# Fewer sweeps and a double-buffered activation tile in a three-stage transformer block on eight cores

## What is computed

```python
x = x + 0.5 * ffn(layernorm(x))
x = x + attn(layernorm(x))[0]      # attn returns x' + cfc_out @ out_w.T + out_b
x = x + 0.5 * ffn(layernorm(x))

def ffn(x):                        # both matrices ternary, activations 8 bit
    h = bit_linear(x, w1)                          # 1024 -> 4096
    h = silu(depthwise_conv1d(h, conv_w, conv_b))  # 3 taps along the sequence
    return bit_linear(h, w2)                       # 4096 -> 1024
def bit_linear(x, w):              # act_quant divides by the row's scale again
    return einsum('bsd,hd->bsh', act_quant(x), weight_quant(w))

def attn(x):                       # layernorm, a state space scan, then per step:
    def step(h, xt):
        cat = concatenate([xt, h], -1)
        ff1 = tanh(cat @ ff1_w.T + ff1_b); ff2 = tanh(cat @ ff2_w.T + ff2_b)
        t = sigmoid((cat @ ta_w.T + ta_b) * 0.1 + (cat @ tb_w.T + tb_b))
        return ff1 * (1 - t) + t * ff2             # h_new
```

## Time and profile before

| | us |
|---|---|
| median of 3 runs (lowest, highest) | 8986.92 (8979.69, 8989.06) |
| the profiled execution | 8987.16 |
| its span, slowest core (core 6) | 8985.6 |
| spans of the 8 cores | 8943.4 to 8985.6 |
| mean granted TensorE clock of the cores | 0.687 to 0.690 |

### The profile page before, as it was taken

The page is one execution under the profiler, slowest core; times in us unless marked ns, Lnnn a source line. Parts: engine busy times, 40 slices in busy tenths (PEclk is TensorE's granted clock), DMA queues, the critical chain, the costliest instruction groups (busy, mean ns, idle before and its releaser), DMA issues. The chain is left out here.

```text
span 8985.6 us, 55001 instructions; the slowest of 8 cores (8943.4 to 8985.6 us)
## 1 busy us (share of the span) xinstructions
PE 3672.7 (41%) x17501; PEld 1967.2 (22%) x17682; DVE 3800.5 (42%) x7133; ACT 2088.6 (23%) x3546; POOL 64.3 (1%) x119
## 2 busy tenths in 40 slices
PE   0223323332333210666322178888832332333257
PEld 0122212221222110323100033333410221222123
DVE  2445454554455441000465444444434545454400
ACT  2222222222222213000000015555510222222200
POOL 0000000000000000000000000000000000000000
PEclk9756655665666555878655589999965665566578
DMA  7000000000000024232111100000033000000132
GB/s 205 31 28 14 14 16 27 14 14 19 24 14 14 24 70 154 82 105 95 56 52 51 64 19 1 1 1 1 1 137 115 14 15 14 28 14 14 33 126 84
DMA packets 310172, 406.89 MB, mean 45 GB/s; under 512 B 20482, under 2 KB 224514, under 8 KB 304130
## 3 DMA queue, kind: packets, MB, share of 16 engines
q1 hardware_dynamic: 296546, 341.50, 12.1%
q0 software_dynamic: 13344, 61.87, 2.2%
HBM read 271.23 MB, written 135.26 MB: 45 GB/s over the span
## 5 line engine op out<-in xcount | busy, mean ns | idle before, releaser
L467 PE MATMUL pb<-xq,wq 128*128 128x258 bf16 x3584 | 660.2, 370 | 1041.7 <-DVE tg L494 659.2
L467 PE MATMUL pb<-xqb,wq 128*128 128x258 bf16 x3072 | 568.2, 371 | 972.2 <-DVE tg L494 596.5
L566 PE MATMUL pb<-yqb,wq 128*128 128x512 bf16 x3511 | 801.8, 389 | 374.7 <-DMA yqb<-yqbuf 249.2
L467 PEld LDWEIGHTS pb<-xq,wq 128*128 128x128 bf16 x3584 | 465.6, 132 | 1241.1 <-issue 1075.0
L486 DVE SCALAR_TENSOR_TENSOR tg<-pb,convws,tg 128x256 f32<-128x256 f32 x832 | 345.1, 478 | 901.3 <-ACT tg L478 887.2
L851 PE MATMUL pb<-cfc,WhS 128*128 128x512 bf16 (+1 forms) x2880 | 677.1, 364 | 87.5 <-DVE cfc L882 47.8
L467 PEld LDWEIGHTS pb<-xqb,wq 128*128 128x128 bf16 x3072 | 400.2, 133 | 1144.7 <-issue 1001.2
L478 ACT ACTIVATE tg<-pb,convbs,convws 128x256 f32<-128x256 f32 x832 | 401.3, 562 | 748.0 <-PE pb L467 546.9
L572 DVE SCALAR_TENSOR_TENSOR yy<-pb,rw2h,xt 128x512 f32<-128x512 f32 x112 | 84.1, 751 | 1091.8 <-PE pb L566 1091.8
L566 PEld LDWEIGHTS pb<-yqb,wq 128*128 128x128 bf16 x3584 | 356.8, 100 | 816.4 <-issue 414.5
L532 DVE TENSOR_TENSOR yqa<-y,pbc 128x256 bf16<-128x256 f32 x832 | 280.3, 414 | 548.1 <-ACT y L527 548.1
(11 more groups left out here) (176 smaller groups left out, 4523.1 us busy)
## 6 DMA issues: line engine op xcount, KB each, us to landing
yqb<-yqbuf SPq DMA_DIRECT2D x9, 4096.0 KB
yqbuf<-yqa SPq DMA_DIRECT2D x34, 1024.0 KB
yqb<-yq2buf SPq DMA_DIRECT2D x5, 4096.0 KB
xt<-xT SPq DMA_DIRECT2D x9, 2048.0 KB
x1buf<-yy SPq DMA_DIRECT2D x9, 2048.0 KB
yq2buf<-yqa SPq DMA_DIRECT2D x18, 1024.0 KB
xta<-xT SPq DMA_DIRECT2D x17, 1032.0 KB
y<-w1T SPq DMA_DIRECT2D x8, 2048.0 KB
```

Of the source, the lines that this page charges most:

```text
L467: mm = T.matmul(pb[j][:, 0:tw], wq[:, kd * HD + mh * P:kd * HD + (mh + 1) * P], xq_t[:, kd * tw:(kd + 1) * tw], start=(kd == 0), stop=(kd ...
L566: mm = T.matmul(bank[:, 0:tw], wq[:, kh * D + md * P:kh * D + (md + 1) * P], yqb[:, kh * tw:(kh + 1) * tw], start=(kh == 0), stop=(kh == H ...
```

## The change

Four things are edited.

1. `NSWEEP` goes from 18 to 15. Since 15 is odd, the states of the last sweep go to the second half of `cfc`, and the output projection reads those of the 14th sweep.
2. Stage A no longer copies the scales into `a2col`.
3. Stage B no longer spreads them: the `tensor_scalar` instructions that fill `repb`, the four transposes and the copy into `a1s` of each tile are gone.
4. Stage B gets two buffers for `yqb`. The load of a tile moves from the SP queue to the GpSimd queue (`G.dma_start`), and that of tile i+1 is issued at the start of tile i, once VectorE and TensorE have finished tile i-1. TensorE waits for `yqb` alone. SP still waits for the last eviction and for the store of `yy`, and then issues `xt`; VectorE waits for it. `xt` and `yy` stay single.

```diff
-NSWEEP = 18
+NSWEEP = 15
...
-                quant_cols(y2, HC, TOA, None, 2,
-                           acol_dst=a2col[:, c0 // 128:c0 // 128 + 2], halves=2)
+                quant_cols(y2, HC, TOA, None, 2, halves=2)
...
-            for c0 in c0list:
-                tw = 512
+            tw = 512
+
+            def load_yqb(ii):
+                yqb = yqbs[ii % 2]
+                sv.wait(G)
+                sp.wait(G)
+                G.wait_ge(sg.h, sg.n) if sg.n else None
+                sg.inc(G.dma_start(
+                    bass.AP(yqb, 0, [[HC * tw, P], [tw, HC], [1, tw]]),
+                    hbm3(yq_hbm, c0list[ii], HC, tw)), 16)
+                return sg.n
+
+            gmark = load_yqb(0)
+            for ti, c0 in enumerate(c0list):
+                yqb = yqbs[ti % 2]
                 sv.wait(SY)
-                dma_fence()
-                sy.inc(SY.dma_start(sb3(xt, DC, tw, tw), hbm3(src_res_hbm, c0, DC, tw)), 16)
-                sy.inc(SY.dma_start(
-                    bass.AP(yqb, 0, [[HC * tw, P], [tw, HC], [1, tw]]),
-                    hbm3(yq_hbm, c0, HC, tw)), 16)
-                colbcast(pbc2, a2col[:, c0 // 128:c0 // 128 + 4], tw, 4)
-                sp.wait(V)
-                V.tensor_copy(a1s[:, 0:tw], pbc2[:, 0:tw])
-                sv.inc(V.drain())
-                sy.wait(T)
-                sy.wait(V)
+                SY.wait_ge(sy.h, sy.n) if sy.n else None
+                sy.inc(SY.dma_start(sb3(xt, DC, tw, tw),
+                                    hbm3(src_res_hbm, c0, DC, tw)), 16)
+                xmark = sy.n
+                sg.wait(T, gmark)
+                sg.wait(V, gmark)
+                sy.wait(V, xmark)
+                if ti + 1 < len(c0list):
+                    gmark = load_yqb(ti + 1)
                 for md in range(DC):
...
-                yqb = sb("yqb", [P, HC * 512], BF16, stb)
+                yqb = [sb("yqb", [P, HC * 512], BF16, stb),
+                       sb("yqb2", [P, HC * 512], BF16, stb)]
```

More of the change, by code:

```diff
@@ L544, in ffn_stage_a, with ffn_stage_b @@
             bar()
-        def ffn_stage_b(wq, xt, yy, yqb, src_res_hbm, c0list, yq_hbm, out_hbm):
-            for c0 in c0list:
-                tw = 512
-                sv.wait(SY)
-                dma_fence()
-                sy.inc(SY.dma_start(sb3(xt, DC, tw, tw), hbm3(src_res_hbm, c0, DC, tw)), 16)
-                sy.inc(SY.dma_start(
-                    bass.AP(yqb, 0, [[HC * tw, P], [tw, HC], [1, tw]]),
-                    hbm3(yq_hbm, c0, HC, tw)), 16)
-                colbcast(pbc2, a2col[:, c0 // 128:c0 // 128 + 4], tw, 4)
-                sp.wait(V)
-                V.tensor_copy(a1s[:, 0:tw], pbc2[:, 0:tw])
-                sv.inc(V.drain())
-                sy.wait(T)
-                sy.wait(V)
+        def ffn_stage_b(wq, xt, yy, yqbs, src_res_hbm, c0list, yq_hbm, out_hbm):
+            tw = 512
[11 more added lines that the diff above has]
+                yqb = yqbs[ti % 2]
+                sv.wait(SY)
+                SY.wait_ge(sy.h, sy.n) if sy.n else None
[7 more added lines that the diff above has]
+                    gmark = load_yqb(ti + 1)
                 for md in range(DC):
                     bank = pb[md % 2]
-                    hb = hmt if md % 2 == 0 else hmt2
                     sev.wait(T, sev.n - 1)
@@ L579, in ffn_stage_b @@
                 sy.inc(SY.dma_start(hbm3(out_hbm, c0, DC, tw), sb3(yy, DC, tw, tw)), 16)
+                stmark = sy.n
             bar()
```

## The result

| | before | after |
|---|---|---|
| median of 8 runs, us (lowest, highest) | 8988.31 (8979.69, 9000.7) | 8614.46 (8599.7, 8626.64) |
| ratio of the two (95% interval) | | 0.9585 (0.9575 to 0.9596) |
| profiled execution: span of the slowest core, us | 8985.6 (core 6) | 8613.0 (core 4) |

The kernel became 374 us faster. 8576 was forecast, within 8450 to 8635: the time lies in the range, 38 us above the number and 4 us above the narrower range of the likeliest case.

What follows compares the result with a forecast made beforehand. Stage B was taken as bound by load, matmuls, store, load strictly in turn, the recurrence by sweeps that nothing covers. Gains of 209 + 2 + 128 + 72 = 411 us gave 8576 us, range 8450 to 8635.

Steps and rivals of the forecast that it cites:

- the likeliest case: Stage B: a stall ahead of the third chunk between the bounds; time 8540 to 8610 us, chance 0.49.
- The sweeps: Recurrence: three sweeps fewer at 69.64 us each, nothing covering them, save 209 us.
- The copies of stage A: Stage A: 26 copies of the scales on its path, 0.08 us each, save 2 us.
- The spread in stage B: Stage B: spreading the scales was covered by loads before, so removing it gains 0.
- Stage B: Both stages B: matmuls run on between tiles, stalling 15 and 11 us ahead of the third chunk; gains 128 and 72 us.
- The price of GpSimd's queue: Stage B: a `yqb` load needs some 17 to 30 of its 70 us, so nothing is charged.
- x: Stage B: time from the store's issue to the landing of `xt`, taken as 27 and 23 us.
- The bounds: Stage B: x between 15.8 and 31.8 us in the first stage, 14.8 and 27.0 in the second.
- The price of sharing: Stage B: store and `xt` each slowed beside GpSimd's load from 7.9 to 12.9 us, together 25.8 us.
- SP's transfers wait out the whole of `yqb`: Rival in stage B: stalls of 19.8 and 15.0 us, gains 94 and 60, time 8622 us; chance 0.22.
- The page's rule on turns: Stage B: DMA engines alternate queues packet by packet; at one row a turn, x is 24 and 20, some 36 us better.
- the page's box on VectorE holding up GpSimd's transfers: Stage B: GpSimd's transfers wait during VectorE's two-port instructions; evictions cost 6 us a tile, so loads would keep their time.

Runs made afterwards that it cites:

- all ahead: Kernel with two buffers for `xt`, changed to 14 sweeps, with SP issuing store, `xt` and `yqb` one behind another, a semaphore each: 8341.75 us, ratio 0.9283.
- `xt` ahead of the store: Changed kernel, but SP issues `xt` after the last eviction and the store right behind, waiting for neither; VectorE waits for both: 8554.23 us, ratio 0.9516.

## Why the prediction was right, and where it was off

**The sweeps** (209 us): right. 1255.0 to 1046.2 us, 208.8.

**The copies of stage A** (2 us): not seen, and too small to be. From the first load of stage A to the first load of w2 the cores' median is 3039.0 us before and 3039.2 after.

**The spread in stage B** (0): right, and the new stall is its cover, by the kernel that puts it back.

**Stage B.** The mechanism came as worked out: no gap between tiles, a stall ahead of the third chunk, released by the eviction that waits for `xt`, the clock at 0.50 behind it, periods of 73 to 75 us in the first stage (73.5 forecast) and 61.5 (62.3) for its last tile. The price of GpSimd's queue was nothing, as taken. By core 6, on which the prediction was worked out, the first stage B went from 789.9 to 667.4 us, a gain of 122 for 128 forecast; but that core was the longest of the eight there, and the median gained 102.

The term that was mis-sized is x, the time from the store to the landing of `xt` (read here up to the first eviction, within about half a microsecond the same). I took 27 and 23 us; core 4 shows 28.4 and 29.6, stalls of 16.45 and 17.64 us for 15 and 11, and periods of about 75 us in the second stage for 69.5. The second stage gained 58 us between the slowest cores (421.9 to 364.4) for 72. Three steps behind x don't hold:

- The bounds. "The buffers of the first stage are slower than those of the second" was read off a tile of core 6 with a near neighbour; core 4 took 27.0 us in the first stage as core 6 did in the second. So 31.8 was no bound, the 4 us between 27 and 23 had no ground, and the 27.0, taken as an upper bound, was passed in both stages.
- The price of sharing. In the row that I took for it the packets of both queues are of 16 KB (127 packets with 2.08 MB and 54 with 0.88 MB from 146 to 156 us); in stage B those of GpSimd are twice as long as those of SP. And the store was hardly slowed (8.4 us) while `xt` took 20.0, where I had put each at 12.9. That their 25.8 comes near the sum of 28.4 is luck.
- The neighbour had no term. With neighbours over 15 us apart x is 26.2 to 27.6 us, which is what the three transfers take one after another where nothing disturbs them (27.0); nearer ones go with up to 4 us more. In the second stage of core 4 they stood 7.6 us apart. That the neighbour is the cause was argued from the table and not tried.

In both stages `xt` lands behind `yqb`. That is the rival "SP's transfers wait out the whole of `yqb`" (8622 us, chance 0.22) in its mechanism, except that the store did not wait. By its own bounds the likeliest case, a stall between them, still came in the first stage (16.45 us of 3.8 to 19.8) and not in the second (17.64 of 2.8 to 15.0). The rival's sum isn't borne out either: it had gains of 94 and 60 us in the two stages, and 126 and 58 were measured between the slowest cores, since its 31.8 has the same fault. That the time lies nearer to 8622 than to my 8576 comes from the output projection.

The page's rule on turns (the Trainium skill, DMA: Bandwidth & Descriptors, "Queues, rings and completion order") agrees with the trace in that the two queues shared the engines packet by packet: 626 of GpSimd's and 660 of SP's in 12 us. Taken as one row a turn, as the prediction tried it, it does not: that would have given x = 24 and 20. The packets of GpSimd were not rows of 1 KB but of 4 KB, so the turns favoured `yqb` and not `xt`. (Ten tiles have a load beside them and not twelve, so that reading was worth 30 us and not 36.) Of the page's box on VectorE holding up GpSimd's transfers (the Trainium skill, SBUF — State Buffer) the trace shows nothing in a stage B: an issue took 1.7 us and its load had landed after 27.4 at most.

**What had no term** is the output projection: +18 us in the median, +22 between the slowest cores. With the 15 us of the second stage B that is 36 of the 38 us. The other differences (8 us gained in "A1 + w2", 5 lost in the load of w1, 2 each in smaller places) nearly cancel. Here too the neighbour is the reading that the table of arrivals supports, and not a shown cause.

**Open.** "A1 + w2" is 3296 to 3299 us in the two kernels with 18 sweeps, 3288 to 3292 with 15 and 3283 with 14. Stage A is the same to 1 us; the difference lies in the quantization of w2, where ScalarE and VectorE wait mostly for its loads (180 and 54 us of idle time from 3300 to 3540 before). Nothing here tells why. Nor was it tried whether setting two neighbours apart on purpose gives the output projection its 18 us back.

## What to carry to other kernels

When one load is taken off the path, ask what the next one in line will share its time with: here the prefetch was issued at the very moment when the two transfers on the path began, it took the larger share of the bytes, and a wait that held it back 16 us was worth 135 us. Put what is needed first and what is needed late on one queue, in that order, or give both a second buffer. Read a period on several cores before building on it: the 91 us of the slowest core were 85 on the others. And check which half of a ping-pong buffer the reader takes before choosing an odd number of passes.

## What the runs showed of the hardware

- Two transfers on one queue of SP passed one behind another (`xt` landed 7.8 us after its issue with 4 MB queued behind it); on the queues of SP and GpSimd they passed side by side, and the one of SP landed last (20.0 us).
- Side by side the two queues passed about as many packets each (660 and 626 in 12 us), of 2 KB on SP's queue and of 4 KB on GpSimd's, so that GpSimd's moved 2.54 MB and SP's 1.35. GpSimd's load of rows of 1 KB had packets of 4 KB.
- The nearer in time two neighbouring cores loaded, the longer it took: 8 MB in 32.0 us at 0.7 us apart, 25.5 us at 20.8 us apart; store to first eviction of a stage B 30.1 to 31.0 us at up to 4 us apart, 26.2 to 27.6 at over 15.
- TensorE's granted clock was seen at a third value beside 0.50 and 1.00, under full load: 0.81, held over 100 us without a gap (all ahead, core 4), with evictions 8.40 us apart instead of 6.91. In two of the 13 profiles four pairs of neighbours show it (all ahead, and `xt` ahead of the store), each time both cores of the pair, while core 6 had 1.00 beside cores 4 and 5.
- In the last 4 us of a gap of 4.5 us the clock was 0.99, and in the 3 us behind it 0.51.
